# Differential attention ordered by a list schedule, with scores in halves in single PSUM banks

## The reference, cut to what matters

```
q, k = rope_rotate(x @ Wq.T), rope_rotate(x @ Wk.T)      # 16 heads of 16
o1 = softmax(q1 @ k1.T * d**-0.25) @ vfull               # 8 heads, vfull is 32 wide
o2 = softmax(q2 @ k2.T * d**-0.25) @ vfull
o  = o1 - lam * o2
o  = o * rsqrt(mean(o*o) + EPS) * ln_w + ln_b
x  = layernorm(x + (o * (1 - LAMBDA_INIT)) @ Wo.T)
```

## Time and profile before

| | |
|---|---|
| median of 3 runs | 3028.58 us (3028.43 to 3034.52) |
| the profiled execution | 3030.09 us |
| its span, first to last instruction | 3028.3 us |
| PE busy | 2859.1 us, 94% |
| DVE, ACT, POOL busy | 72%, 53%, 35% |
| mean granted clock of TensorE | 0.98 |
| stage c, first scores matmul to last c_w | 563.2 to 1621.9 us |

### The profile page before, as it was taken

The page is one execution under the profiler, slowest core; times in us unless marked ns, Lnnn a source line. Parts: engine busy times, 40 slices in busy tenths (PEclk is TensorE's granted clock), DMA queues, the critical chain, the costliest instruction groups (busy, mean ns, idle before and its releaser), DMA issues.

```text
span 3028.3 us, 52408 instructions
## 1 busy us (share of the span) xinstructions
PE 2859.1 (94%) x20384; PEld 1934.4 (64%) x20384; DVE 2171.4 (72%) x5057; ACT 1611.7 (53%) x2976; POOL 1049.2 (35%) x1210
## 2 busy tenths in 40 slices
PE   7898999999999999999998799999999899999997
PEld 5676886533343333333334678888888788888886
DVE  6777345677778778777884677777776577887874
ACT  2221332454655555555565566666667566666662
POOL 3333342113212411221142344444454453444441
PEclk9999999999999999999999899999999999999998
DMA  3000001131322032122212000000010000000001
GB/s 103 2 2 2 28 4 20 18 38 12 37 24 27 6 43 22 17 26 33 25 39 75 24 5 4 5 5 5 12 32 15 27 26 5 12 11 12 11 11 58
DMA packets 46795, 66.63 MB, mean 22 GB/s; under 512 B 10174, under 2 KB 34772, under 8 KB 46548
## 3 DMA queue, kind: packets, MB, share of 16 engines
q1 hardware_dynamic: 46548, 63.29, 11.8%
HBM read 24.99 MB, written 8.39 MB: 11 GB/s over the span
## 4 chain that ended last, share of the span: by engine, by line
PE 72%; DVE 15%; DMA 5%; ACT 3%; POOL 2%; issue 1%; SPq 1%; POOLq 0%; ACTq 0%; DVEq 0%
PE ps L1274 16%; PE pw L121 12%; PE ps L121 10%; PE pw L1250 9%; DMA e_hs<-x 4%; PE ps L1054 4%; PE ps L1434 4%; PE pw L1054 3%; DVE a_am L1770 3%; PE pw L1347 2%; PE pw L1385 2%; PE ps L1238 1%; PE pw L1204 1%; PE pw L1367 1%; DVE stat L1713 1%
## 5 line engine op out<-in xcount | busy, mean ns | idle before, releaser
L1559 ACT ACTIVATE c_p<-pw 128x1024 f32<-128x1024 f32 x512 | 522.6, 1021 | 429.4 <-PE ps L1238 350.6
L1846 DVE TENSOR_REDUCE c_mx<-ps 128x1 f32<-128x512 f32 x1024 | 658.5, 683 | 123.2 <-PE ps L1238 119.8
L1274 PE MATMUL ps<-c_p,c_v 128*64 128x512 f32 x2048 | 555.1, 620 | 7.8 <-DVE c_mr L1859 7.3
L1238 PE MATMUL ps<-c_kst,c_qst 48*128 48x512 f32 x1024 | 386.0, 451 | 6.9 <-DMA c_kst<-shared 3.5
L1250 PE MATMUL pw<-c_qst,c_kst 50*128 50x512 f32 x1024 | 377.0, 447 | 0.8 <-DVE c_v L1819 0.8
L1250 PEld LDWEIGHTS pw<-c_qst,c_kst 50*128 50x128 f32 x1024 | 152.3, 185 | 314.3 <-issue 302.0
L1612 ACT ACTIVATE e_sm<-e_sm,e_mx 128x256 f32<-128x256 f32 x512 | 253.8, 498 | 62.2 <-DVE e_mx L1990 61.9
L2110 POOL TENSOR_SCALAR stat<-stat 128x1 f32<-128x1 f32 (+1 forms) x138 | 31.2, 226 | 719.0 <-DVE stat L1716 429.5
L121 PE MATMUL pw<-shared,e_xb 128*128 128x512 f32 x792 | 218.0, 414 | 2.3 <-DVE e_xb L1939 1.6
L2215 POOL TENSOR_TENSOR e_ss<-e_ss,half 128x16 f32<-128x16 f32 x64 | 186.8, 2918 | 87.3 <-DVE e_ss L1947 70.1
L1274 PEld LDWEIGHTS ps<-c_p,c_v 128*64 128x64 f32 x2048 | 103.0, 135 | 165.8 <-issue 128.3
(11 more groups left out here) (309 smaller groups left out, 6137.6 us busy)
## 6 DMA issues: line engine op xcount, KB each, us to landing
c_qst<-shared SPq DMA_DIRECT2D x192, 64.0 KB
c_kst<-shared SPq DMA_DIRECT2D x192, 64.0 KB
x<-in_L_attn_x SPq DMA_DIRECT2D x8, 512.0 KB, 8.7
keep<-x SPq DMA_DIRECT2D x8, 512.0 KB, 4.5
e_raw<-keep SPq DMA_DIRECT2D x8, 512.0 KB, 3.5
out<-x SPq DMA_DIRECT2D x8, 512.0 KB, 5.9
e_hs<-x SPq DMA_DIRECT2D x64, 63.5 KB
e_raw<-in_L_ffn_w SPq DMA_DIRECT2D x10, 248.0 KB
```

The costliest lines, as they stand in the source:

```text
L1238: e.matmul(bank_of("c_max", n, sh, qt, h), c_qst[i][p0:p0 + 48, sh // 2, 128 * qt:128 * qt + 128], c_kst[i][p0:p0 + 48, sh // 2, 512 * h:5 ...
L1274: ins = e.matmul(pv[64 * h:64 * h + 64, :], c_v[b % 2][:, kt, 33 * hd:33 * hd + 64], p[:, 512 * h:512 * h + 512], start=kt == 0, stop=kt = ...
L1559: e.activation(c_p[kt % 2][:, :], wides[slot["c_s", (n, sh, kt)]], ACT.Exp, scale=0.5).then_inc(SC, 1)
L1846: e.tensor_reduce(c_mx[m % 2][:, qt, h:h + 1], bank_of("c_max", n, sh, qt, h), AX.X, ALU.max).then_inc(VE, 1)
```

## The change

- Stage c is planned by the list scheduler, moved out of stage d into a class Order, with due times DUE_C, a slope PACE = 16.57 us per map, an allowance NEAR = 0.17, a lag of 0.22 after PE and 0.06 after the others, and 0.09 added where PE changes its kind of work. weigh(), its helpers, and prepare() go.
- Scores are taken in halves: c_s(n, sh, kt, h) is one matmul into one bank and one Exp of 128x512. Banks 5, 6, 7 hold scores, banks 0, 1, 4 maxima, banks 2 and 3 the rest as before. Each scores half still goes with the maxima half 32 halves ahead.
- c_p has four buffers instead of two. c_v has one instead of two, so that c_val of block b waits for the c_w of the last map of block b - 1 with the same kt, and each c_w waits for its own c_val alone.
- The DMAs of c_row are a step of their own (row_in) on SP, which the scheduler places; d_tabs has semaphores of its own.
- In stage d the lag before d_exp is applied to the same step only; else its rules are the same.

```diff
+PACE, NEAR = 16.57, 0.17
+DUE_C = {"pe c_s": -2.7, "act c_s": 13.8, "dve c_max": 12.3, "dve c_mm": -8.4, "c_row": -19.7, "row_in": -24.9,
+         "c_stack": -4.2, "pe c_w": 4.4, "act c_o": 21, "pe c_ft": -11.4, "dve c_ft": -13.3, "pool c_ft": 35.8,
+         "c_n": -28.1, "c_val": -1, "c_x": -2.2, "c_rot": 161.5, "pool c_sum": 132.2, "pool c_part": 146.5,
+         "c_ot": 8, "c_wo": 40.4, "n_c": 22.3}
...
+        "pe c_s": 0.34, "act c_s": 0.6, "dve c_max": 0.67, "pe c_row": 0.12,
...
+        "pe c_w": 0.92, "act c_o": 0.56, "pe c_ft": 0.46, ...
...
-                c_v = [sbin(c, f"c_v{i}", [128, 8, 296]) for i in range(2)]
-                c_p = [sbin(c, f"c_p{i}", [128, S]) for i in range(2)]
+                c_v = sbin(c, "c_vals", [128, 8, 336])
+                c_p = [sbin(c, f"c_p{i}", [128, S]) for i in range(4)]
...
-            wide.idle = [(k, tuple(a for b in (4 + 2 * k, 5 + 2 * k) for a in bank.drop(b)[1])) for k in range(2)]
-            pvb = [bank.drop(2)]
+            while late:
+                rows()
+            sbank.idle.append(bank.drop(4))
+            scores.idle = [bank.drop(k) for k in (5, 6, 7)]
...
+            order = Order(P, NEAR, {"pe": 0.22}, 0.06, 0.09)
...
+                def place(t):
+                    P.add("c_s", *i, pe=1)
+                    if later:
+                        P.add("c_max", *later, pe=1)
+
+                op(at(m, "pe c_s", kt + h / 2), "pe", "c_s", i, 1, after + ([("pe", "c_s", *before)] if q else []), takes, place=place,
+                   mode="pair")
+                op(at(m, "act c_s", kt + h / 2), "act", "c_s", i, 1, [("pe", "c_s", *i)] + ([("act", "c_s", *before)] if q else []),
+                   [(weighed, "c_p", *maps[m], kt)] * (1 - h), [(scores, "c_s", *i)])
...
+                    for j in range(4):
+                        i, kt = (b, nb, j), 4 * nb + j
+                        op(at(16 * b, "c_val", kt), "pe", "c_val", i, 1, [("dve", "c_x", b, nb, k) for k in range(2)] +
+                           [("pe", "c_w", *maps[16 * b - 1], kt)], [(bank, "c_val", *i)])
...
+            def turned_rows(b):
+                gone, before = [("dma", "c_stack", 4 * b - 1, sh) for sh in range(4)], []
...
+                        m, t = 16 * (b - 1) + 2 * nb + qk, (b, nb, qk)
...
-            def c_s0(n, sh, kt):
...
-                half_of_s(0, n, sh, kt)
...
-            def c_s(n, sh, kt):
-                half_of_s(1, n, sh, kt).then_inc(PE, 1)
...
+                e.matmul(bank_of("c_s", n, sh, kt, h), c_kst[i][p0:p0 + 50, sh // 2, 128 * kt:128 * kt + 128],
+                         c_qst[i][p0:p0 + 50, sh // 2, 512 * h:512 * h + 512],
+                         start=True, stop=True, skip_group_check=True).then_inc(PE, 1)
...
-                w.wait_ge(*dve("c_val", b, 1, 3))
-                w.wait_ge(*act("c_s", n, sh, kt))
+                w.wait_ge(*dve("c_val", b, kt // 4, kt % 4))
+                w.wait_ge(*act("c_s", n, sh, kt, 1))
...
-                e.activation(c_p[kt % 2][:, :], wides[slot["c_s", (n, sh, kt)]], ACT.Exp, scale=0.5).then_inc(SC, 1)
+                e.activation(c_p[slot["c_p", (n, sh, kt)]][:, 512 * h:512 * h + 512], bank_of("c_s", n, sh, kt, h), ACT.Exp,
+                             scale=0.5).then_inc(SC, 1)
```

More of the change, by code:

```diff
@@ L455, in rows @@
                 n, sh, _ = late.pop(0)
-                P.land(f"row{n % 2}{sh}", 2, "c_row", n, sh)
                 P.use(bank, "dve", "c_row", n, sh, pe=1, act=1, dve=1)
[L459 to L561, removed]
@@ L624, in plan_c @@
[L624 to L628, removed]
-                    if b > 0:
-                        back += [project(b - 1, q) for q in range(8)]
-                if k == 14 * 64:
-                    back.append(prepare())
-                if k % 256 == 137 and b < 3:
-                    back.insert(0, rotated(b + 1))
-                advance(back if later else post)
-                if k % 256 == 255:
-                    while back:
-                        advance(back)
@@ L641, in plan_c @@
+            for b in range(4):
+                for u in range(4 if b < 3 else 3):
+                    normalised(b, u)
+                for q in range(8 if b < 3 else 0):
+                    projected(b, q)
+                if b:
+                    rows_of(b)
+                    turned_rows(b)
+            next_layer()
+            order.run(1e8)
+            assert not order.blocked and not order.ready, (list(order.blocked)[:9], [(o["eng"], o["kind"], o["i"]) for o in order.ready])
             P.add("d_begin")
@@ L693, in run @@
-            def run(until):
-                while ready:
-                    times = [starts(o) for o in ready]
-                    first = min(times)
-                    if first >= until:
-                        return
-                    t, _, k = min((o["due"], k, k) for k, o in enumerate(ready) if times[k] <= first + EPS)
-                    o, t = ready.pop(k), times[k]
-                    for r, kind, *v in o["takes"]:
-                        P.take(r, kind, *v)
-                    ref = (o["eng"], o["kind"], o["i"])
-                    engine_at[o["eng"]] = over_at[ref] = t + o["took"]
-                    if o["place"]:
-                        o["place"](t + o["took"])
-                    else:
-                        P.add(o["kind"], *o["i"], **{o["eng"]: o["n"]})
-                    for r, kind, *v in o["gives"]:
-                        r.give(slot[kind, tuple(v)], (o["eng"], o["kind"], *o["i"]))
-                        r.idle.sort(key=room_at)
-                    settle([ref])
+            order = Order(P, EPS, {}, LAG)
@@ L1532, in c_row @@
                 if m >= 3:
-                    w.wait_ge(*dma("c_row", *maps[m - 3]))
+                    w.wait_ge(*dma("row_in", *maps[m - 3]))
                 w.wait_ge(*pe("c_row", n, sh))
```

320 lines of the change are left out of this document (233 added, 87 removed).

## The result

| | median us | lowest to highest | runs |
|---|---|---|---|
| before | 3028.51 | 3026.03 to 3034.52 | 4 |
| after | 3054.88 | 3049.86 to 3056.13 | 4 |

The ratio is 1.0081, with a 95% interval of 1.0062 to 1.0100: slower by 26 us where 2990 was forecast, and outside the range. The profiled execution took 3049.86 us, with a span of 3047.7.

The account below looks back on a forecast made before the run. PE was taken to bound stage c, with 56.5 us of waiting and slow clock; less 22 left, plus 4 for paired c_w, 38.5 us won: 3030.09 to 2991.6, median 2990 us, range 2970 to 3022.

Parts of the forecast that it names:

- SP and its DMAs ... 0 us: SP's queue in stage c: same DMAs issued, row_in behind a c_stack waits some 5 us, rows ready nearly a map early; 0 us.
- A stop costs more than its length: PE in stage c: behind a 3.12 us stop a scores matmul takes 0.79 us in place of 0.49, the clock having fallen.
- c_rot later: Block borders: c_rot's chain takes 21 us against some 18, so maxima may wait; bounds 0 to 3 us, 2 taken a border.
- One values buffer: Three block borders: c_val must follow the old block's last c_w of its kt; bounds 0 to 5 us, 1 taken a border.
- Halves on PE, 0 us: Scores in halves: PE issues the same matmuls in the same pairs, 0 us if pieces keep 0.33; ACT's additional Exp time hidden.
- rival 1: Stage c steps cost what the plan assumes, 1.78 us in place of 1.67: 3046, or 3027 if partly true; chance 0.10.
- Semaphores, 0 us: PE in stage c: 512 more increments, one for each score half, cost 0 us by the trace.
- rival 2: The skill's semaphore rule holds, about 26 ns for each added increment on PE: 13.5 us more, 3004; chance 0.06.
- c_w next to c_w, 4 us: PE in stage c: two c_w in a row save up to 0.05 us each, 0 to 26 us; few such neighbours, 4 taken.
- A third bank for maxima: Stage c: one more half of slack, about 0.68 us, covers most DVE bursts; the 10.6 us in 29 waits nearly goes.
- New waits, 0 us: ACT and DVE: c_x waits for the previous block's c_val, c_n2 for an older c_n3; both ended maps earlier, 0 us.
- Rival 3: Block borders, slower: c_val exposed and last c_rot's rows late, 19.4 us in place of 3 each: 3039; chance 0.07.

Follow-up runs that it names:

- e12: Kernel after with only SP's order changed, seven row DMAs moved ahead of stacks, other engines' order untouched: 3019.19 us, ratio 0.9969 to before.
- e1: Kernel after with the plan's c_stack price on SP raised from 4.1 to 6.7 us and row_in due at -400: 3001.41 us, ratio 0.9908 to before.
- e3: Kernel after with c_rot and its POOL parts due two maps (33.1 us) earlier, prices unchanged: 3043.03 us, ratio 1.0049 to before.
- e8: On top of e1, two banks for maxima and four for scores, still in halves: 3001.42 us, ratio 0.9906 to before.
- e7: On top of e1, two weights buffers (c_p) in place of four: 3054.91 us, ratio 1.0089 to before.
- e9: On top of e1, c_rot and POOL parts due 8 us earlier, stacks held behind rows in some maps only: 2998.12 us, ratio 0.9900 to before.
- e10: On top of e1, c_rot, c_sum and c_part due 8 us earlier: 2998.72 us, ratio 0.9906 to before.

## Why the prediction was wrong, step by step

**The step that failed is "SP and its DMAs ... 0 us".** It read "the same 384 c_stack DMAs and 128 row DMAs are issued", and a late row was priced at one stack, "some 5 us", covered by nearly a map of slack. The count was right. That the queue's order changed was not followed: up to five stacks in a row, 32 us, against a slack of a map. In the trace of after it cost 25.3 us of stops, in e12 the order of SP alone gives 35.7 us back, and with the price and the rows' due time 53 come back. The trace of before had what was needed: the earlier trace rows shows the first three DMAs of a stack, 2.39 us, its other three take 3.56 more, so 6.0 in all, and the plan's table says 4.1. I compared the plan's PE and ACT prices to rows and not this one.

**A stop costs more than its length** was said of the earlier trace rows, but given no term except at c_rot's bound. After to e1, 23.4 us of stops took 48.9 us of stage with them; after to e12, with PE's order the same, 13.9 took 30.8. No fixed factor follows: e3 has 6.3 us more of stops than after and a stage 8.1 us shorter, since four of its seven stops are of 8.5 to 9 us and the time at 1.2 GHz is 30.7 us less. In after, the clock stood at 1.2 GHz for 6.8 us behind a stop of 1.7 and for 10.2 behind the one of 8.95.

**The start** was put at 7 us and left alone. It held the longest stop of all, 8.95 us in map 2.

**c_rot later**, 2 us a border with the bound 0 to 3: measured 1.7. Right, in its mechanism too (the maxima wait for the last c_kst). **One values buffer** at 1 us a border was never seen as a stop on its own, and no run took it back; map 16 of e1, with its c_val, took 22.1 us, which is an undisturbed map of 14.3 and c_val's 7.2, so 0.6 over.

**Halves on PE, 0 us**: still 0.33, hence rival 1 (the plan's 1.78 a step) falls. The groups of stage c in after show the ACT side: an Exp of 512 is 0.595, so two are 1.19, above my 1.14 (line, shapes, count | busy, mean ns | idle time before).

```profile
L1622 ACT ACTIVATE c_p<-pw 128x512 f32<-128x512 f32 x1024 | 562.0, 595 | 373.3 <-PE ps L1305 193.8 <-PE pw L1305 92.6 <-PE pw L1322 64.7
```

ACT idles 373 us in front of them, so they are hidden as said.

**Semaphores, 0 us**: the half has an increment more and takes 0.33 as before. The median spacing of two such halves is 0.336 us before and 0.337 in after, so rival 2 falls too. By the Trainium skill (TensorE: Matmul & The Clock Gate, The cost: per-tile semaphore tail) the added increment would have made every second half 0.026 us longer and the stage 13.5 us, an estimate from the page; the measurement decides against it for these pairs.

**c_w next to c_w, 4 us**: the right sum, from two wrong factors. The saving is 0.15 a pair and not 0.05 for each c_w (two c_w in a row take 1.87 in place of 2.02, below); there were some 30 pairs, 4.5 us.

```profile
625.71 1.94 PE L1335 MATMUL ps<-c_p,c_vals 128*64 128x512 f32 x8 [0.29 <-DVE c_t L1956]
627.58 0.49 PE L1322 MATMUL pw<-c_qst,c_kst 50*128 50x512 f32 x1
```

**A third bank for maxima, "this wait nearly goes"**: with the bank it does, from 10.6 us in 29 waits to 3.2 in 4 in e1, and without it little of it does, 8.4 in 19 (e8). That it bought time is not shown, since e8 is as fast. **The order and four buffers**: this is what carries the gain; c_p's ring was mentioned in passing, and with e1's due times it is worth 53 us (e7), twice what e1 gains on the kernel before.

**New waits, 0 us**: DVE's 5.5 us for POOL and with it PE's 4.6 were not foreseen. My "POOL has work for 245 us only" is an average; four weight splits of 1.9 us stood in a row ahead of the norm's step. Why the list put them there wasn't tried.

**The rivals.** Rival 3, slower through the block borders, came nearest: 3039 where 3055 was measured. Its place and one of its two queues ("because POOL or SP is busy with ... row DMAs") were right, though it was stacks that held rows, not rows that held stacks. Its price of 19.4 us a border was about double the 8.4 us of stops at the first, before the clock's share, and it knew nothing of the start. With a chance of 0.07 it had too little, since "against" named what PE could fill in and POOL's average load, and never the length of SP's queue.

**What was right** shows once the queue is mended: stage c is 1033.0 us in e1 and 1026.8 in e9, against 1020 forecast, and the kernel 3001 and 2998 against 2990. The gain of 38.5 us was 27 to 30. PE was to be idle for less than 12 us of the stage: it was for 41.5 in after, 18.3 in e1 and 13.8 in e9.

## What to carry to other kernels

When a scheduler takes over a queue that was ordered by hand, check each of its prices against the trace of before, DMA issues included, and write out the order of that queue around its bursts; equal counts say nothing. A DMA that gates the bounding engine goes ahead of every transfer that nothing needs yet. Moving work earlier on one engine can bunch it on another, so look at the queue behind it. A stop of the bounding engine costs more than its length where its clock falls with it: the stage of after lost about twice the sum of its stops, and in e3, with longer ones, less than that. A small DMA issued by a computing engine isn't free either: it holds that engine for its whole issue.

## What the runs showed of the hardware that I had not expected

- Issuing a DMA from SP costs more when others are in front of it: in after the three 64 KB DMAs that open a stack take 2.2 to 2.6 us of issue after a pause or a row, and each later three 2.7 to 3.9 us (0.7 to 0.9 against 0.9 to 1.3 each).
- Two c_w in a row take 0.91 and 0.96 us of PE where one alone takes 1.01, so a change between the kinds of matmul costs some 0.1 us beside what four pieces cost.
- e7 stands idle for 32.5 us in stage c, in short waits, and is never at 1.2 GHz; e10 stands idle for 16.8 with a few stops over 1 us and is there for 30.7 us. The sum of idle time does not tell what the clock does, and neither does the length of the stops alone: e7 has one of 1.94 us with no 1.2 GHz behind it, four of 1.38 to 1.44 us in e10 are followed by 3.4 to 6.8 us of it and one of 1.47 by none, and e12 has 10.2 us of it from 1370.4 us on with no stop above 0.51 us just before. What decides it is open.
